# Transposed tokens laid out image by image: one 128 by 192 product per image for scores and router, and two banks in turn for the last expert products

## The reference, cut to what matters

```python
# layer 0: tokens of an image (64 from a wavelet transform, 128 of text), b = image
x = concat(tokens, text)                                  # [16, 192, 64]
n = layernorm(x)
scores = einsum('bnd,bmd->bnm', n, n) / sqrt(64)          # 192 x 192 for each image
x = x + softmax(scores) @ n
f = layernorm(x)
weights = f @ wr + br                                     # the router: one number a token
idx = top_k(weights, 96); sel_idx = idx[:, :95]           # capacity 0.5
y = (gelu(f[sel_idx] @ w1 + b1) @ w2 + b2) * weights[sel_idx]
x = (x + f) with y added at sel_idx
# layer 1: window attention with 16 query heads, one key head, rope and RMS norms
# then a top-1 choice among 32 experts (64 -> 16 -> 64, relu), added to x
```

## Time and profile before

| what | value |
|---|---|
| three timed runs | 514.03, 513.05, 510.72 us, median 513.05 us |
| the profiled execution | 511.42 us, of which span 509.6 us |
| granted TensorE clock over the span | 0.99 |
| TensorE busy | 458.2 us of the span (90%) |
| VectorE, ScalarE, GpSimd busy | 344.3, 315.6, 235.7 us |
| one pair in the steady middle | 55.7 us (router products start at 159.21, 214.84, 270.55 us) |

### The profile page before, as it was taken

The page is one execution under the profiler, slowest core; times in us unless marked ns, Lnnn a source line. Parts: engine busy times, 40 slices in busy tenths (PEclk is TensorE's granted clock), DMA queues, the critical chain, the costliest instruction groups (busy, mean ns, idle before and its releaser), DMA issues.

```text
span 509.6 us, 14274 instructions
## 1 busy us (share of the span) xinstructions
PE 458.2 (90%) x5771; PEld 360.2 (71%) x5771; DVE 344.3 (68%) x1151; ACT 315.6 (62%) x675; POOL 235.7 (46%) x266
## 2 busy tenths in 40 slices
PE   7887898989998999989998999889998999789985
PEld 3444577777877878767876787777876787667763
DVE  3588779757995599568975799568956795344220
ACT  2337475767767676787666866778568657463322
POOL 3347733674347634653457525772475246620010
PEclk9999999999999899999999999999999899899999
DMA  8350240023101320033002310132003200231000
GB/s 299 107 99 1 49 96 2 2 44 71 23 10 22 65 44 4 2 82 65 3 4 42 64 32 3 23 65 51 10 3 83 45 3 3 42 72 30 3 1 9
DMA packets 13969, 21.38 MB, mean 42 GB/s; under 512 B 5024, under 2 KB 6544, under 8 KB 13776
## 3 DMA queue, kind: packets, MB, share of 16 engines
q1 hardware_dynamic: 13904, 20.47, 17.3%
HBM read 5.07 MB, written 0.79 MB: 11 GB/s over the span
## 4 chain that ended last, share of the span: by engine, by line
PE 40%; DVE 31%; ACT 14%; POOL 8%; issue 6%; DMA 1%; POOLq 0%; ACTq 0%; DVEq 0%
PE bank L1083 30%; PE bank L1116 9%; DVE negm L695 5%; DVE q_sb L630 4%; DVE tb L630 4%; DVE ssq L646 3%; POOL qs L879 2%; DVE on L712 2%; ACT qT L904 2%; POOL q_sb L872 1%; DMA qM<-mT 1%; ACT qs L904 1%; ACT L1036 1%; ACT xf L915 1%; POOL rsA L806 1%
## 5 line engine op out<-in xcount | busy, mean ns | idle before, releaser
L837 POOL TENSOR_TENSOR q_sb<-q_sb,tb 128x1024 f32<-128x1024 f32 x24 | 57.2, 2385 | 94.5 <-DVE tb L630 94.5
L695 DVE TENSOR_REDUCE negm<-bank 128x2 f32<-128x384 f32 (+2 forms) x112 | 68.1, 608 | 39.3 <-PE bank L1083 38.8
L904 ACT ACTIVATE qT<-bank 128x512 fp32r<-128x512 f32 x96 | 52.4, 597 | 42.8 <-PE bank L1116 42.0
L1083 PE MATMUL bank<-kS,qM 128*128 128x224 f32 (+3 forms) x384 | 64.8, 285 | 7.7 <-issue 4.4
L1083 PEld LDWEIGHTS bank<-kS,qM 128*128 128x128 f32 x384 | 55.0, 194 | 21.8 <-issue 8.6
L879 POOL TENSOR_TENSOR qs<-q_sb,qs 128x1024 fp32r<-128x1024 f32 x24 | 56.7, 2362 | 27.9 <-ACT qs L904 27.7
L1083 PE MATMUL bank<-vx,p 128*64 128x65 f32 x1024 | 65.4, 223 | 0.0
L1036 ACT ACTIVATE p<-bank 128x512 f32<-128x512 f32 x96 | 54.7, 592 | 12.6 <-PE bank L1083 12.3
L1083 PEld LDWEIGHTS bank<-vx,p 128*64 128x64 f32 x1024 | 57.3, 138 | 0.0
L1083 PE MATMUL bank<-qT,kh 128*128 128x512 f32 (+1 forms) x128 | 51.7, 445 | 2.2 <-ACT p L1036 1.2
L1116 PE MATMUL bank<-ident_r,qs 128*128 128x128 f32 x384 | 44.8, 258 | 3.8 <-POOL qs L879 2.7
(11 more groups left out here) (177 smaller groups left out, 1025.4 us busy)
## 6 DMA issues: line engine op xcount, KB each, us to landing
qM<-qT SPq DMA_DIRECT2D x48, 256.0 KB, 3.2
qM<-qM SPq DMA_DIRECT2D x1, 1280.0 KB, 9.3
wts<-weights SPq DMA_DIRECT2D x1, 1059.0 KB, 5.9
p<-masks SPq DMA_DIRECT2D x1, 960.0 KB, 9.8
h<-txt SPq DMA_DIRECT2D x1, 672.0 KB, 7.1
img<-images SPq DMA_DIRECT2D x8, 72.0 KB, 2.2
q_sb<-wqkv SPq DMA_DIRECT2D x1, 576.0 KB, 8.0
p<-experts SPq DMA_DIRECT2D x1, 512.0 KB, 10.3
```

Of the source, the lines that this page charges most:

```text
L695: ve.tensor_reduce(dst, src, AX_X, ALU.max, negate=True).then_inc(s_vec, 1)
L837: return gp.tensor_tensor(a, a, b[:, :, ::-1], ALU.add)
L904: return ac.activation(dst, src, ACT.Copy)
L1083: return pe.matmul(dst, lhsT, rhs, start=start, stop=stop, skip_group_check=True)
```

## The change

1. `a_xt` transposes tiles in the order 0, 2, 1. The columns of `xaT` are then image 0 (192) and image 1 (192), each in one piece. Image 0's late 64 stand behind its 128, image 1's before its 128.
2. `a_s01` and `a_route` are one product of 128 weight columns by 192 for each image, without `halves` (2 instead of 8 products for a pair, each). `a_s2` is one product of 64 by 192 for each image (2 instead of 4).
3. What reads them follows: slices in `a_ctx`, `a_y`, `a_rank1`, and `before` has 512 instead of 384 columns in the DMA `cst<-shapes`.
4. In the last pair `h1` and `h3` go to bank 5 (`h_bank`), and `h1`, `h2`, `h3` wait for the ScalarE step two before instead of the one before. The six idle products before `h1`, `h2`, `h3` (two each) are gone; those before `out` remain.
5. `MERGE` and `WARM` are new tables. 260 of TensorE's 712 steps stand at another place, at most 12 places away; 177 of 497 on ScalarE, 123 of 463 on VectorE, 22 of 145 on GpSimd.

```diff
-        0): 6, ("B", "q00", 0): 1, ("B", "kv", 0): 5, ("A", "xT1", 1): 10, ("A", "s2", 1): 4, ("A", "ctx", 1): 1,
+        0): 6, ("B", "q00", 0): 1, ("B", "kv", 0): 5, ("A", "s01", 1): 6, ("A", "s2", 1): 3, ("A", "ctx", 1): 6, ("B",
...
+        def h_bank(p, c):
+
+            return bank[BANK_E[0] if p.n == PAIRS - 1 and c % 2 else BANK_D]
...
-                    transposes(bA, [src[:, t, 0:D] for t in range(NT)], ident, a_pe)
+                    transposes(bA, [src[:, t, 0:D] for t in (0, 2, 1)], ident, a_pe)
...
                 for b in range(2):
-                    c0, c1 = cols(b)
-                    halves(bA[:, T * b:T * b + P], xaT[:, c0], xaT[:, c0], True, True)
-                    ins = halves(bA[:, T * b + P:T * b + T], xaT[:, c0], xaT[:, c1], True, True)
+                    ins = mm(bA[:, image(b)], xaT[:, own(b)], xaT[:, image(b)], True, True)
                 ins.then_inc(a_pe, 1)
...
-                for k in range(2):
-                    for b in range(2):
-                        key = cols(b)[k]
-                        q = slice(64 * b, 64 * b + 64)
-                        ins = mm(dst[q, P * k:[P, T][k]], xaT[:, cols(b)[1]], xaT[:, key], True, True)
+                for b in range(2):
+                    q = slice(64 * b, 64 * b + 64)
+                    ins = mm(dst[q, 0:T], xaT[:, P + 64 * b:P + 64 * b + 64], xaT[:, image(b)], True, True)
...
                 for b in range(2):
-                    c0, c1 = cols(b)
-                    halves(bA[:, T * b:T * b + P], wt("wr"), xfT[:, c0], True, True)
-                    ins = halves(bA[:, T * b + P:T * b + T], wt("wr"), xfT[:, c1], True, True)
+                    ins = mm(bA[:, image(b)], wt("wr"), xfT[:, image(b)], True, True)
...
             def d_h(c):
                 def f(p):
-                    pe.wait_ge(d_act, after(D_ACT, p, ["oneT", "h0", "h1", "h2"][c]))
+                    pe.wait_ge(d_act, after(D_ACT, p, ["oneT", "h0", "h1", "h2"][max(0, c - 1) if p.n == PAIRS - 1 else c]))
                     if p.n == 0 and c == 0:
                         pe.wait_ge(set_e1, 2)
-                    mm(bD[:, 0:PT], e1_hi[:, P * c:P * c + P], xdT[:, :], True, False)
-                    mm(bD[:, 0:PT], e1_lo[:, P * c:P * c + P], xdM[:, :], False, True).then_inc(d_pe, 1)
+                    o = h_bank(p, c)[:, 0:PT]
+                    mm(o, e1_hi[:, P * c:P * c + P], xdT[:, :], True, False)
+                    mm(o, e1_lo[:, P * c:P * c + P], xdM[:, :], False, True).then_inc(d_pe, 1)
```

More of the change, by code:

```diff
@@ L41 @@
 MASK_COLS = dict(maskS=KEYS, maskE=KEYS_E, hot=NH * BLOCK)
-SHAPE_COLS = dict(rope=288, iota=32, before=384)
+SHAPE_COLS = dict(rope=288, iota=32, before=512)
 FIRST_COLS = dict(ident=128, resize=32, own_j=8, tok=64, tokb=64)
@@ L147 @@
 W_ORDER = ["eye", "mask", "wq0", "wq1", "wq2", "wq3", "e1"]
-WARM = {("A", "rows", 0): 7, ("A", "tok", 0): 1, ("A", "xT1", 0): 14, ("A", "s01", 0): 1, ("A", "ctx", 0): 6, ("A",
+WARM = {("A", "rows", 0): 7, ("A", "tok", 0): 1, ("A", "xT1", 0): 14, ("A", "s01", 0): 1, ("A", "ctx", 0): 5, ("A",
         "xT2", 0): 16, ("A", "route", 0): 1, ("A", "y", 0): 6, ("A", "rows", 1): 4, ("A", "tok", 1): 1, ("B", "xT",
[5 rows of a table removed]
[4 rows of a table added]
 FILL = {}
@@ L556, in _ @@
             halves = [(slice(0, P), 0, 0, 0), (slice(0, P), 1, 1, 0), (slice(0, 64), 0, 2, 1), (slice(64, P), 1, 2, 1)]
-            before = cs("before").rearrange("q (k s) -> q k s", k=2)
+            seen = cs("before").rearrange("q (k s) -> q k s", k=2)
+            before = [seen[:, :, HALF:HALF + T], seen[:, :, 0:T]]
             rt = bA[:, 0:2 * T].rearrange("q (b t) -> q b t", b=2)
@@ L565, in a_rank1 @@
                 for t in range(2):
-                    ve.tensor_tensor_reduce(junk[t], rt[:, t, 0:P], ident, 1.0, 0.0, ALU.mult, ALU.add,
+                    ve.tensor_tensor_reduce(junk[t], rt[:, t, HALF * t:HALF * t + P], ident, 1.0, 0.0, ALU.mult, ALU.add,
                                             wcol[:, t:t + 1])
-                ve.tensor_tensor_reduce(junk[2].rearrange("q (k s) -> q k s", k=2), rt[:, :, P:T],
-                                        ident.rearrange("q (k s) -> q k s", k=2), 1.0, 0.0, ALU.mult, ALU.add,
+                ve.tensor_tensor_reduce(junk[2], bA[:, P:2 * P], ident, 1.0, 0.0, ALU.mult, ALU.add,
                                         wcol[:, 2:3]).then_inc(a_vec, 1)
@@ L574, in a_rank2 @@
                 for q, b, t, k in halves:
-                    ins = ve.scalar_tensor_tensor(eq[q, t, :], rt[q, b, :], wcol[q, t:t + 1], before[q, k, :],
+                    ins = ve.scalar_tensor_tensor(eq[q, t, :], rt[q, b, :], wcol[q, t:t + 1], before[b][q, k, :],
                                                   ALU.is_equal, ALU.mult)
@@ L1054, in f @@
                         copy(xdM[0:D, :], bD[0:D, 0:PT])
-                    ac.activation(dst, src, func, **kw).then_inc(d_act, 1)
+                    ac.activation(dst, src if src is not None else h_bank(p, int(name[1]))[:, 0:PT], func, **kw).then_inc(d_act, 1)
                 return f
@@ L1076, in _ @@
                 ("D", "oneT"): d_do("oneT", xdM[D:P, :], bD[D:P, 0:PT]), ("W", "e1"): w_e1,
-                **{("D", f"h{c}"): d_do(f"h{c}", hmT[:, c, :], bD[:, 0:PT], ACT.Relu, bias=wt("eb1")[:, c:c + 1]) for c in range(4)}})
+                **{("D", f"h{c}"): d_do(f"h{c}", hmT[:, c, :], None, ACT.Relu, bias=wt("eb1")[:, c:c + 1]) for c in range(4)}})
         @block.tensor
@@ L1146, in f, with image, own @@
                     wait_apart(pe, a_act, after(A_ACT, p, wait))
-                    transposes(bA, [src[:, t, 0:D] for t in range(NT)], ident, a_pe)
+                    transposes(bA, [src[:, t, 0:D] for t in (0, 2, 1)], ident, a_pe)
                 return f
-            def cols(b):
-                return slice(P * b, P * b + P), slice(2 * P + HALF * b, 2 * P + HALF * b + HALF)
+            def image(b):
+                return slice(T * b, T * b + T)
+            def own(b):
+                return slice(2 * P * b, 2 * P * b + P)
+            late = slice(P, 2 * P)
             def a_s01(p):
@@ L1179, in a_ctx @@
                 for b in range(2):
-                    halves(bA[:, w * b:w * b + w], pA01[:, b, 0:P], xa[:, b, :], True, False)
-                    halves(bA[:, w * b:w * b + w], pA2[:, 0:P], xpad[:, b, :], False, True)
+                    halves(bA[:, w * b:w * b + w], pA01[:, b, 64 * b:64 * b + P], xa[:, b, :], True, False)
+                    halves(bA[:, w * b:w * b + w], pA2[:, 64 * b:64 * b + P], xpad[:, b, :], False, True)
                 for b in range(2):
                     q = slice(64 * b, 64 * b + 64)
-                    mm(bA[q, 2 * w:3 * w], pA01[:, b, P:T], xa[:, b, :], True, False)
+                    mm(bA[q, 2 * w:3 * w], pA01[:, b, P - P * b:P - P * b + HALF], xa[:, b, :], True, False)
                 for b in range(2):
                     q = slice(64 * b, 64 * b + 64)
-                    ins = mm(bA[q, 2 * w:3 * w], pA2[:, P:T], xpad[:, b, :], False, True)
+                    ins = mm(bA[q, 2 * w:3 * w], pA2[:, P - P * b:P - P * b + HALF], xpad[:, b, :], False, True)
                 ins.then_inc(a_pe, 1)
@@ L1214, in a_y @@
                     for c in range(2):
-                        ins = halves(bank[a_bank(p, "y")][:, D * t:D * t + D], h1T[:, c, P * t:P * t + P], w2[:, c, :], c == 0, c == 1)
+                        ins = halves(bank[a_bank(p, "y")][:, D * t:D * t + D], h1T[:, c, P * (0, 2, 1)[t]:P * (0, 2, 1)[t] + P], w2[:, c, :], c == 0, c == 1)
                 ins.then_inc(a_pe, 1)
@@ L1492, in shape_constants @@
     own = np.stack([row, P + row % HALF], 1)[:, :, None]
-    c["before"] = (j < own).reshape(P, 2 * T)
+    seen = (j < own).astype(np.float32)
+    c["before"] = np.concatenate([seen[:, :, P:T], seen], 2).reshape(P, 2 * (T + HALF))
     c["resize"] = np.concatenate([haar_resize(), np.zeros((P - IMG, 32))], 0)
```

## The result

The changed kernel took 519.3 us (median of 20 runs, 514.07 to 522.75); the kernel before, in the same session, 513.28 us (20 runs, 510.72 to 515.81). The ratio is 1.0086, with a 95% interval of 1.0058 to 1.0113: slower by 4.4 us by the ratio and by 6.0 us by the medians. 510.9 us had been forecast, and 514.0 us as the upper end; a time over 518.2 us had been given a chance of 0.03.

What follows compares the result with a forecast made beforehand. TensorE, busy 90% of the span, was taken as the bound, with program ends and single waits beside it. From 512.7 us, 0 + 0.6 - 0.4 - 2.0 + 0 = -1.8 gave 510.9 us; range 507.0 to 514.0.

Steps and rivals of the forecast that it cites:

- The order tables: Whole program: 260 TensorE steps stand elsewhere, moved only short distances, neither adding nor removing work; 0, with ±2 us.
- The clock: Last stretch, in a rival: without the six idle products the clock may fall before out, giving back 1.9 us; chance 0.10.
- The end, -2.0 us: Last pair's expert products: two banks let products overlap Relus, so out begins at 501.99 instead of 504.00; bounds 0 and -2.1.
- The product itself: Router, s01 and s2: fewer products stream as many columns, a 192-column pass taking 0.16 us; about zero.
- The rank, +0.6 us: Pairs three to eight: V8 0.20 us later delays the rank and h1a; three waits of 0.20 counted, bounds 0 and +1.2.
- the net 0.2 us of the forecast: Full-array form's total cost from mode changes: +0.6 us at the rank and -0.4 us in the first two pairs.
- the modes cost more: Rival, router between V7 and V8: its covers vanish, costing 0.55 us in each of six pairs, 3.3 us; 513.6 us, chance 0.12.
- The first two pairs, -0.4 us: First two pairs: fewer mode changes and one idle product fewer ahead of ctx; -0.4 us, bounds -0.8 and +0.3.
- the new order gains in the middle: Rival, middle pairs: the new order fills 0.8 us of waits in each of six pairs, -4.8 us more; 506 us, chance 0.15.
- The end doesn't deliver: Rival, last pair: the clock falls before out, or the two banks don't overlap; 512.8 us, chance 0.10.
- the signs of being wrong: Middle period moving over 0.4 us from 55.7 a pair, 192-column passes far from 0.16 us, or the last slice's clock falling.

Runs made afterwards that it cites:

- e2: The kernel before with the changed kernel's order tables and idle products, keeping two idle products each before h1 to h3: 516.46 us, ratio 1.0046.
- e4: The kernel before with only the two banks for the last pair's expert products, without the six idle products there: 511.74 us, ratio 0.9957.
- e3: The changed kernel with the first 33 steps of VectorE's order and first 5 of GpSimd's as before: 514.66 us, ratio 1.0019.
- e7: The changed kernel with 9 and 10 more idle products inside TensorE's two waits in the head: 513.93 us, ratio 1.0031.
- e6: The changed kernel, new order included, with s01 and the router as two half-array products over the same 192 columns: 515.98 us, ratio 1.0055.
- e1: The changed kernel with the order tables and idle products of before, without the six ahead of h1 to h3: 513.97 us, ratio 1.002.
- e9: e4 with 8 idle products in TensorE's wait ahead of the last pair's S0: 511.68 us, ratio 0.9947.
- e5: e1 with s01 and the router as two half-array products over the same 192 columns: 511.09 us, ratio 0.9958.
- e8: The changed kernel with only the first 5 steps of GpSimd's order as before (masks' casts back): 516.72 us, ratio 1.0059.
- e10: e1 with s01 as half-array products, the router alone full: 513.22 us, ratio 0.9983.
- e11: e1 with the router as half-array products, s01 alone full: 513.05 us, ratio 0.9977.
- e12: The changed kernel with only the first 33 steps of VectorE's order as before: 517.08 us, ratio 1.004.

## Why the prediction was wrong

**The step that failed is "The order tables ... I take 0 for them, with ±2 us".** It argued from TensorE alone: how far its steps move, how many changes of mode there are, how much it waits in a pair. The two moves that cost the most are not on TensorE. They are steps on VectorE and GpSimd, of whose 123 and 22 moved steps the prediction looked at none. The price of these two isn't the time that the long operation takes: it is what it does to a short one on the other engine that runs beside it. The runs showed 3.5 us of lateness by 35 us in place of the 0 (1.5, of which 0.3 stood before the collision, and 2.0, in e2 against e4), of which 2.6 us were still there at 336 us, although e4 had had a fall of the clock on the way and e2 none; e2 has +3.4 us at full clock against the kernel before, and putting the head's steps back (e3) took 4.6 us off the change. The bound of ±2 was worked out from the middle, where indeed little happened: 1.7 us from 107 to 327 us, with one clock fall of 3.4 us in either trace.

**The clock** stood in the prediction as a rival for the end alone. The change runs at 0.978 against 0.986, which is 2.9 us at the slope above, about half of the 6.0 us between the medians. In its trace the clock is down for 30.7 us, against 10.3 us in the kernel before: 6.8 us in the head, 6.8 at 73 us, 3.4 at 186 us and 13.6 between 449 and 466 us. e7, changed in the head alone, is back at 0.987; why the end of the program follows, no run shows.

**The end, -2.0 us:** right in size (2.1 us in the traces, 1.8 to 2.2 us timed) and in how.

**The product itself:** passes of 192 columns behave as taken. The router's step to V8 is 0.13 us longer than with the old columns and 0.15 longer than with halves of 192, where 0.20 had been forecast.

**The rank, +0.6 us:** right: +0.7, in four waits of 0.17 each, in the order of before. In the new order there are six such waits, and 6.4 us in the change, 5.6 us with halves (e6): the order adds 2.1 us to the 3.5 of the earlier trace rows, the form 0.8. What I missed is that this is not all: the form costs 1.4 to 1.8 us at full clock, and that lies between the net 0.2 us of the forecast and the 3.3 us of the rival "the modes cost more" (chance 0.12), under the 2.4 us at which it was to decide. The rival's mechanism, 0.55 us in each of six pairs, is not what happened: the waits for the rank grew by 0.7 us in all (0.8 in the new order).

**The first two pairs, -0.4 us:** not there. Between 24 and 56 us, e1 runs within 0.2 us of e4 and of the kernel before. (e1 keeps six idle products ahead of `ctx`, so the 0.22 us for the sixth is not in this; the parts named there also add up to -0.5, not -0.4.)

**The rivals:** "the new order gains in the middle" (0.15) is out by its main condition, since the order loses. In the middle it gains nothing either: e2 is 3.4 us behind e4 at 107 us and 2.6 at 336, and e4 had one fall of the clock between (1.4 us). "The end doesn't deliver" is out. No rival had a loss in the head, and neither had the signs of being wrong: in the change passes of 192 columns start 0.16 us apart, the last slice's clock is full, and the pairs from 168.66 and 224.97 us last 56.3 and 55.8 us (55.6 and 55.7 before), the longer one with a fall of the clock in it. No run shows that the layout by image, to which the diff gave the most lines, moved anything.

## What to carry to other kernels

When a change brings a new order, list every moved step on every engine and ask what runs beside it at its new place. Between VectorE and GpSimd an operation of 1.3 us made a 0.2 us operation last 1.2 us, and three casts made three small `tb` last 2.0 us more. Few of the operations that ran side by side here did this, so look in the trace for one that is longer than others of its form. Where a chain makes TensorE wait 2 us in front of busy work, price the clock behind the wait too (0.5 to 1.7 us for a fall of 3.4 us here), and try idle products in it; in e9 they did nothing. And take a change apart before judging it: the two banks alone give 0.9957 (0.9926 to 0.9988), a gain that the rest of this change hid.

## What the runs showed that was not expected

A small transfer is complete only with the last of its sixteen parts, and in eight traces one part came late while a load of code was under way. `qM<-mT` moves 8 KB, and TensorE needs it in the first pair near 66 to 72 us. In six of the fourteen traces it landed 1.9 us after its issue and TensorE waited 0.3 us; in six, the change among them, 3.0 to 3.3 us and TensorE waited 1.4 to 1.8 us; e5 and e6 lie between. DMA of the changed kernel from 62 to 72 us (KB each, median us to landing), and its TensorE and queues at that place:

```profile
qM<-mT SPq DMA_DIRECT2D x1, 8.0 KB, 3.3
```

```profile
68.53 0.58 SPq L432 DMA_DIRECT2D qM<-mT  x1
...
71.87 0.73 PE L1086 MATMUL bank<-qT,kh 128*128 128x512 f32 x2 [1.73 <-DMA qM<-mT]
```

and from 68.5 to 72 us by queue (packets, MB, share of 16 engines):

```profile
q8 instruction: 1, 0.02, 2.3%
```

That one packet is a load of 16 KB of instructions, from 69.46 to 70.74 us. Fifteen of the transfer's completions stand in the trace at 70.12 to 70.37 us, the sixteenth at 71.83. In e7 the load ran from 65.65 to 66.93, ahead of the transfer, and all sixteen stand at 68.68 to 68.95. In e3, e8, e10, e11 and e12, too, a load lies across the transfer and the sixteenth completion is 1.1 to 1.5 us behind the fifteenth; in e5 and e6 a load lies across it and the last is 0.6 and 0.4 us behind. In the other six traces no load does, and it is at most 0.01 us behind. In the change, e8 and e12 the clock then fell for 6.8 us, which is about another 2 us. That the load is what delays the sixteenth part is read from their times in these traces; no run moved the load alone. If it holds, an edit that shifts the code or the time by a microsecond can win or lose 1.5 to 3.5 us in a place that it does not touch: 3.5 us of the change's lateness are of this kind, and 3.8 us of e7's lead over it. A part of what stays open above may be this too.
